# Second layer: dispatch and projections in one stage, the dispatch cut into pieces between the half chunks

## The chip, the cores and the metric

The kernel runs on one core of one Trainium2 chip. The metric is the device time of one execution in microseconds, the median of three runs. Five engines have queues of their own and meet only at semaphores: PE (TensorE, matmuls), DVE (VectorE), ACT (ScalarE), POOL (GpSimd) and SP (SyncE, which issues most DMAs). "SPq" and "PEq" in the rows are the queues of the engines, in which issues and waits stand.

## What is computed

A block of four layers over 4 batches of 1024 tokens with 128 features; each layer is x + s * g, s an attention-like part and g an activated feed-forward part, both of the normalized x. The change lies in the second layer (L1), in what comes first there: the projections of the attention, and the router of the feed-forward part with 8 experts, of which each token takes two.

```python
qkv = x @ W_qkv + b_qkv                       # attention, 16 heads of 8
q, k, v = jnp.split(qkv, 3, axis=2)
...
logits = xf @ Wg + bg                         # feed-forward, xf = x as 4096 rows
w = jax.nn.softmax(logits, axis=-1)
top_w, top_idx = jax.lax.top_k(w, K)          # K = 2 of 8
top_w = top_w / (top_w.sum(axis=-1, keepdims=True) + EPS_GATE)
```

## The kernel before

The kernel is a row of stages. Each (`Stage`) has its own buffers and semaphores and ends with a barrier of all engines, so that nothing of the next begins before the last DMA of the stage has landed. x is held as 32 tiles of 128 tokens, its normalized form turned as `xnT` (128 features by 4096 tokens).

**dispatch1** (`dispatch_stage`, L1789) reads `xnT` and writes three maps to memory: where each row goes (`send`), its weight (`pick_weight`) and the expert of each block of 128 rows (`owner`). SP loads the router's weights, then stores 4.7 MB of zeros over `sorted_x`, from a tile that DVE clears and into which GpSimd writes row numbers. PE makes 32 tiles of logits, each with 128 columns of `xnT` as weights and only 8 moving columns. DVE does all else in one chain (`link`: each instruction waits for the one before): softmax with ACT's Exp, comparison of every pair of experts (five instructions over 2048 elements, L1900 to L1905), a mask, then a wait for two matmuls of PE that count the mask, then running sums over the tiles, slots, weights and owners. SP stores the maps:

```python
            sp.wait_ge(zeroed, NZ * DMA)
            for n, (dst, src) in enumerate(((send_d, send_i), (weight_d, wsel), (expert_d, owner_i))):
                sp.wait_ge(maps_ready, n + 1)
                sp.dma_start(dst[:], src[:]).then_inc(stored, DMA)
...
            for t in range(NT):
                last = mm(lg[:, t, :], xnT[:, t * P:(t + 1) * P], wr[:], start=True, stop=True)
            last.then_inc(logits, 1)
            pe.wait_ge(mask_ready, 1)
```

**proj1** (`project_l1`, L2160) makes q, k and v. A chunk is 512 tokens; PE makes three fills for each, q, k and v (24 in all), into a ring of four PSUM slots. q and k are stored as three bf16 parts whose sum is the float value. Per half chunk m (q or k of a chunk, 16 in all): ACT writes the first part (`first_part`), DVE the remainder (`remainder`, L2247), ACT the second part of it (`second_part`), DVE the third (`third_part`, L2254). v only gets its bias on DVE (`values`, L2258). PE may fill a slot again when ACT and DVE have read it. SP stores q, k and v for each batch of two chunks, ten DMAs a batch. The next stage, attn1, starts with loads of q and k.

Of the kernel before, what the change touches and what calls it, by code (L numbers as in the profile page):

```python
# [7 lines left out]
I32 = mybir.dt.int32  # L8
# [5 lines left out]
P = 128  # L14
D = 128
# [885 lines left out]
def broadcast_rows(vec, n=P):  # L901

    return vec.partition_broadcast(n)
# [1256 lines left out]
def project_l1(nc, xnT, w_qkv, b_qkv, q_d, k_d, v_d):  # L2160
# [4 lines left out]
    SLOTS = 4  # L2165
    with Stage(nc, "proj1") as st:
        w, b_col, bv_b = st.sb("w", [P, 3 * D]), st.sb("b_col", [P, 2]), st.sb("bv_b", [P, D])
# [4 lines left out]
        consts, made, high, rested, middle, low, v_ready, stored = (  # L2172
            st.sem(n) for n in ("consts", "made", "high", "rested", "middle", "low", "v_ready", "stored"))
        block = st.block()

        @block.sync
        def _(sp):
            sp.dma_start(w[:], w_qkv).then_inc(consts, DMA)
# [16 lines left out]
            sp.wait_ge(stored, DMA * n)  # L2195

        @block.tensor
        def _(pe):
            pe.wait_ge(consts, 4 * DMA)
            for n in range(N):  # L2200
# [8 lines left out]
                if j < 2:  # L2209
                    last = nc.tensor.matmul(ps[:, n % SLOTS, :], w[:, j * D:(j + 1) * D], xnT[:, c * CH:(c + 1) * CH],  # L2210
                                            start=True, stop=True)
                else:
                    for t in range(TPC):
                        last = nc.tensor.matmul(ps[:, n % SLOTS, t * P:(t + 1) * P], xnT[:, (c * TPC + t) * P:(c * TPC + t + 1) * P],
                                                w[:, 2 * D:3 * D], start=True, stop=True)
                last.then_inc(made, 1)

        @block.scalar
        def _(act):
            def first_part(m):  # L2220
                c, j = divmod(m, 2)
                act.wait_ge(made, 3 * c + j + 1)
# [10 lines left out]
            for m in range(2 * NCH):  # L2233
                if m + 1 < 2 * NCH:
                    first_part(m + 1)
                second_part(m)

        @block.vector
        def _(dve):
            V = nc.vector  # L2240

# [14 lines left out]
            def values(c):  # L2256
                dve.wait_ge(made, 3 * c + 3)
# [3 lines left out]
            dve.wait_ge(consts, 4 * DMA)  # L2261
            remainder(0)
            for m in range(2 * NCH):
# [4 lines left out]
                third_part(m)  # L2268

# [756 lines left out]
def recurrent_block_kernel(nc, a, out):  # L3026
# [15 lines left out]
    with ExitStack() as ctx:  # L3042
# [33 lines left out]
        dispatch(1, "top2", BLOCKS, "Wg bg")  # L3076
        project_l1(nc, xnT, a["L1_attn_W_qkv"], a["L1_attn_b_qkv"], q1, k1, v1)
# [41 lines left out]
```

## Time and profile before

| | us |
|---|---|
| median of three runs | 3577.64 (3575.88 to 3577.95) |
| profiled execution, time | 3574.13 |
| its span | 3572.4 |
| dispatch1, SP's first issue to that of proj1 | 1859.69 to 1911.32 |
| proj1, to SP's first issue of attn1 | 1911.32 to 1959.42 |

Times in the rows are microseconds from the start of the span. PE is busy for 80% of the span, DVE for 66%, ACT for 52%, GpSimd for 42%. In a row of the timeline, the brackets say how long the engine had stood idle before the row and what it had waited for; "x8" is a number of instructions, merged into one row. A float32 matmul stands twice in the trace.

### The profile page before, as it was taken

Reading aid. Unit: us, or ns where it says so; the run is one execution under the profiler, and the core shown is the slowest. Engines: PE = TensorE matmul, PEld = TensorE weight load, DVE = VectorE, ACT = ScalarE, POOL = GpSimd, SP = SyncE. Lnnn points to the kernel's source line nnn. Section 1 sums busy time; section 2 is a strip of 40 time slices with the busy share of each in tenths; the row PEclk is TensorE's granted clock in tenths of the full one; section 3 lists DMA queues with packets and bytes.
Section 4 is the critical chain, followed back from the end, with each engine's and each line's share of the span. In section 5 each row is a group of like instructions: output and inputs, shape, how many; then the busy total and the mean of one; then the engine's idle time right before and its main releaser. Section 6 shows DMA issues by size and latency. Waiting matters only on the chain. (4 is left out here: it accounts for less than half of the span.)

```text
span 3572.4 us, 66799 instructions
## 1 busy us (share of the span) xinstructions
PE 2857.9 (80%) x21131; PEld 1282.4 (36%) x21132; DVE 2354.1 (66%) x3384; ACT 1843.7 (52%) x2985; POOL 1515.6 (42%) x1109
## 2 busy tenths in 40 slices
PE   3999999999999978599943799999969820384993
PEld 1333333333333328333331122222246520252771
DVE  5666666666666637788866999999823358134663
ACT  2555555555555540344462599999934350144431
POOL 0989989999998980100000010110126604560000
PEclk9999999999999988799966799999989955696995
DMA  2011111111111115200013222222121123113002
GB/s 83 30 45 42 54 41 46 54 41 46 49 46 46 40 45 202 85 1 0 0 55 103 42 58 50 53 53 54 46 83 46 36 79 115 40 40 87 10 12 64
DMA packets 265381, 189.65 MB, mean 53 GB/s; under 512 B 149056, under 2 KB 210872, under 8 KB 264322
## 3 DMA queue, kind: packets, MB, share of 16 engines
q1 hardware_dynamic: 257154, 174.25, 17.2%
q0 software_dynamic: 8128, 14.18, 1.2%
q8 instruction: 50, 0.82, 0.1%
q14 instruction: 49, 0.40, 0.0%
HBM read 105.28 MB, written 67.62 MB: 48 GB/s over the span
## 5 line engine op out<-in xcount | busy, mean ns | idle before, releaser
L331 POOL TENSOR_TENSOR attn_esum<-attn_esum,attn_prob 128x1024 f32<-128x1024 f32 x384 | 904.0, 2354 | 31.1 <-ACT attn_prob L482 7.4
L553 DVE TENSOR_REDUCE attn_half_max<-attn_peek 128x2 f32<-128x1024 f32 x512 | 627.4, 1225 | 399.1 <-PE attn_peek L382 395.3
L482 ACT ACTIVATE attn_prob<-attn_score 128x1024 f32<-128x1024 f32 x512 | 512.4, 1021 | 247.8 <-PE attn_score L365 247.8
L848 ACT ACTIVATE attn_prob<-attn_score 128x512 f32<-128x512 f32 x1024 | 556.3, 596 | 72.1 <-PE attn_score L798 58.0
L865 DVE TENSOR_REDUCE attn_half_max<-attn_peek 128x2 f32<-128x1024 f32 x512 | 583.6, 1217 | 10.8 <-PE attn_peek L784 10.7
L412 PE MATMUL attn_acc<-attn_prob,attn_v 128*64 128x512 f32 x2048 | 487.9, 597 | 0.1
L814 PE MATMUL attn_acc<-attn_prob,attn_v 128*32 128x256 f32 x4096 | 327.8, 392 | 12.0 <-ACT attn_out L840 10.5
L1779 POOL DMA_INDIRECT sorted_x<-attn_sent_rows,attn_send x64 | 62.6, 978 | 555.0 <-PE attn_score L798 520.3
L784 PE MATMUL attn_peek<-attn_ke,attn_qe 48*128 48x512 bf16 x1024 | 202.8, 393 | 47.0 <-DMA attn_ke<-k 32.3
L382 PE MATMUL attn_peek<-attn_hi 64*128 64x512 f16 x1024 | 200.2, 388 | 34.2 <-DVE attn_half_max L553 34.2
L798 PE MATMUL attn_score<-attn_qe,attn_ke 49*128 49x512 bf16 x1024 | 200.6, 389 | 7.7 <-ACT attn_prob L848 5.8
L2134 DVE TENSOR_TENSOR experts_pre<-experts_up,experts_b 128x512 f32<-128x512 f32 x112 | 77.5, 692 | 193.8 <-PE experts_up L2064 193.8
L331 POOL TENSOR_TENSOR attn_esum<-attn_prob 128x1024 f32<-128x1024 f32 x64 | 151.1, 2361 | 126.7 <-ACT attn_prob L482 126.7
L412 PEld LDWEIGHTS attn_acc<-attn_prob,attn_v 128*64 128x64 f32 x2048 | 130.8, 137 | 201.0 <-issue 156.4
L1583 PE MATMUL experts_up<-experts_x,experts_up_w 128*128 (+1 forms) x816 | 198.3, 379 | 1.5 <-DVE experts_down_w L1672 1.5
L367 PE MATMUL attn_score<-attn_hi 64*128 64x512 f16 x1024 | 195.1, 378 | 0.0
L367 PE MATMUL attn_score<-attn_lo,attn_hi 64*128 64x512 f16 x1024 | 195.1, 378 | 0.0
L367 PE MATMUL attn_score<-attn_hi,attn_lo 64*128 64x512 f16 x1024 | 194.9, 377 | 0.0
L365 PE MATMUL attn_score<-attn_shift,attn_sel 64*128 64x512 bf16 x1024 | 194.8, 377 | 0.0
L1845 POOL MEMSET dispatch_before<- 128x64 f32 x2 | 0.3, 151 | 457.9 <-POOLq L41 457.9
L1649 ACT ACTIVATE experts_a<-experts_up 128x512 f32<-128x512 f32 x136 | 81.2, 597 | 157.0 <-PE experts_up L1583 154.0
L2034 POOL DMA_INDIRECT picked<-experts_y,experts_result x112 | 115.7, 1033 | 88.0 <-POOL experts_y L2031 85.3
(451 smaller groups left out, 4539.0 us busy)
## 6 DMA issues: line engine op xcount, KB each, us to landing
attn_xb<-attn_x_all SPq DMA_DIRECT2D x66, 256.0 KB, 2.5
attn_invB<-inv SPq DMA_DIRECT2D x64, 256.0 KB, 3.9
o<-attn_out SPq DMA_DIRECT2D x32, 512.0 KB, 2.7
out_o<-o SPq DMA_DIRECT2D x8, 2048.0 KB
mix_f<-picked SPq DMA_DIRECT2D x16, 512.0 KB, 7.2
experts_x<-sorted_x SPq DMA_DIRECT2D x112, 65.0 KB
attn_qe<-q SPq DMA_DIRECT2D x192, 32.0 KB
attn_ke<-k SPq DMA_DIRECT2D x192, 32.0 KB
```

The source lines that it names most:

```text
L331: nc.gpsimd.tensor_tensor(own, before, prob[:, u % NPROB, :, :], ALU.add).then_inc(added, 1)
L367: last = mm(score[:, u % 2, h, :], ks[r, slot, WHICH["k"], keys], qs[r, slot, WHICH["q"], queries], start=(n == 0), stop=False)
L382: last = mm(peek[:, h, :], hi[r, slot, WHICH["q"], t * P:(t + 1) * P], hi[r, slot, WHICH["k"], half * CH:(half + 1) * CH], start=True, sto ...
L412: last = mm(acc[rows_of(h), :], v[:, slot, t, rows_of(h)], prob[:, u % NPROB, h, :], start=(t == 0), stop=(t == KT - 1))
L482: nc.scalar.activation(prob[:, u % NPROB, :, :], score[:, u % 2, :, :], ACT.Exp).then_inc(exped, 1)
L553: V.tensor_reduce(half_max[:, half, :, t], peek[:], AX.X, ALU.max, negate=True).then_inc(maxed, 1)
L784: last = mm(peek[:, m % NPEEK, n, :], qe[r, slot, pair, t * P:(t + 1) * P], ke[r, slot, pair, half * CH:(half + 1) * CH], start=True, stop ...
L798: last = mm(score[:, (PAIR * k + n) % RING, :], ke[r, slot, pair, t * P:(t + 1) * P], qe[r, slot, pair, c * CH:(c + 1) * CH], start=True, ...
L814: last = mm(acc[h * COL:(h + 1) * COL, cols], v[:, slot, t, h, :], prob[:, (HG * s + h) % NPROB, cols], start=(t == 0 and p == 0), stop=(t ...
L848: nc.scalar.activation(prob[:, n % NPROB, :], score[:, n % RING, :], ACT.Exp).then_inc(exped, 1)
L865: V.tensor_reduce(half_max[:, half, PAIR * pair:PAIR * (pair + 1), t], peek[:, m % NPEEK, :, :], AX.X, ALU.max, negate=True).then_inc(maxe ...
L1583: ins = nc.tensor.matmul(out, ws[pw][:, cols], xs[px][own], start=start and n == 0, stop=stop and n == 2)
```

## The change

`dispatch1` and `proj1` become one stage, `dispatch_and_project_stage`; the second dispatch of the kernel (third layer) stays as it was. SP loads both sets of weights, the projection's first, stores the zeros, then q, k and v as before. GpSimd clears the tile of zeros and, from its own queue, stores the three maps. On PE the logit tiles stand in four pieces of eight, each followed by a fill, and the two counting matmuls in front of fill 12. ACT's Exp follows the second part of half chunk 2. DVE's work of the dispatch is cut into eight pieces, which are the old instructions in nearly the old order (the weights come before the running sums, the slots after them); between them stand one or two steps of the projection.

```diff
 
-def project_l1(nc, xnT, w_qkv, b_qkv, q_d, k_d, v_d):
+def dispatch_and_project_stage(nc, xnT, w, bias, blocks, xs_d, send_d, weight_d, expert_d, w_qkv, b_qkv, q_d, k_d, v_d):
...
         @block.sync
+            sp.dma_start(wq[:], w_qkv).then_inc(consts, DMA)
             for j in range(2):
                 sp.dma_start(b_col[:, j:j + 1], column(b_qkv[j * D:(j + 1) * D])).then_inc(consts, DMA)
             sp.dma_start(bv_b[:], broadcast_rows(b_qkv[2 * D:3 * D])).then_inc(consts, DMA)
+            sp.dma_start(wr[:], w).then_inc(router_in, DMA)
+            sp.dma_start(bias_b[:], broadcast_rows(bias)).then_inc(router_in, DMA)
+            sp.wait_ge(zero_made, 2)
+            for n in range(NZ):
+                sp.dma_start(xs_d.rearrange("(n p r) d -> n p (r d)", n=NZ, p=P)[n], zero[:].rearrange("p r d -> p (r d)")).then_inc(zeroed, DMA)
...
+            sp.wait_ge(zeroed, NZ * DMA)
             sp.wait_ge(stored, DMA * n)
+
+        @block.gpsimd
+        def _(pool):
+            nc.gpsimd.memset(zero[:], 0.0).then_inc(zero_made, 1)
+            pool.wait_ge(zero_made, 1)
+            nc.gpsimd.iota(zero[:, :, D:D + 1].bitcast(I32), [[0, blocks // NZ], [0, 1]], base=NOWHERE, channel_multiplier=0
+                           ).then_inc(zero_made, 1)
...
+            pool.wait_ge(built, 4)
...
+            for n, (dst, src) in enumerate(((send_d, send_i), (weight_d, wsel), (expert_d, owner_i))):
+                pool.wait_ge(maps_ready, n + 1)
+                pool.dma_start(dst[:], src[:]).then_inc(maps_stored, DMA)
+            pool.wait_ge(maps_stored, 3 * DMA)
 
...
+            def fill(n):
...
+            def score_tiles(h):
+                for t in range(h * NT // 4, (h + 1) * NT // 4):
+                    last = mm(lg[:, t, :], xnT[:, t * P:(t + 1) * P], wr[:], start=True, stop=True)
+                if h == 3:
+                    last.then_inc(logits, 1)
+
+            def count():
+                pe.wait_ge(built, 6)
+                pe.wait_ge(mask_ready, 1)
+                flat = mask[:].rearrange("p t e -> p (t e)")
+                mm(ranked[:, 0, :, :].rearrange("p t e -> p (t e)"), earlier[:], flat, start=True, stop=True)
+                mm(tallied[:, 0, :, :].rearrange("p t e -> p (t e)"), ones[:], flat, start=True, stop=True).then_inc(counted, 1)
+
+            pe.wait_ge(consts, 4 * DMA)
+            for n in range(3):
+                fill(n)
+            pe.wait_ge(router_in, 2 * DMA)
+            for h in range(4):
+                score_tiles(h)
+                fill(3 + h)
+            for n in range(7, N):
+                if n == 12:
+                    count()
+                fill(n)
 
         @block.scalar
         def _(act):
             def first_part(m):
                 c, j = divmod(m, 2)
-                act.wait_ge(made, 3 * c + j + 1)
+                act.wait_ge(filled, 3 * c + j + 1)
                 nc.scalar.activation(part[0][:, j, c * CH:(c + 1) * CH], ps[:, (3 * c + j) % SLOTS, :], ACT.Identity, bias=b_col[:, j:j + 1]
                                      ).then_inc(high, 1)
 
@@ -2234,10 +2311,19 @@
                 if m + 1 < 2 * NCH:
                     first_part(m + 1)
                 second_part(m)
+                if m == 2:
+                    act.wait_ge(shifted_ready, 1)
+                    nc.scalar.activation(score[:], shifted[:], ACT.Exp).then_inc(exped, 1)
...
+            def scores():
+
+                dve.wait_ge(router_in, 2 * DMA)
+                dve.wait_ge(logits, 1)
+                link(V.tensor_tensor(score[:], lg[:], per_expert(bias_b), ALU.add))
+                link(V.reduce_max(red[:], score[:], AX.X))
+                V.tensor_tensor(shifted[:], score[:], per_tok(red), ALU.subtract).then_inc(shifted_ready, 1)
...
+            def softmax():
+                dve.wait_ge(built, 6)
+                dve.wait_ge(exped, 1)
+                link(V.reduce_sum(red[:], score[:], AX.X))
...
+            def equals():
+                link(V.tensor_tensor(pair2[:], sj, si, ALU.is_equal))
...
+            def larger():
+                link(V.tensor_tensor(pair[:], sj, si, ALU.is_gt))
...
+            def ranks():
+                link(V.reduce_sum(rank[:], pair[:], AX.X))
+                V.tensor_scalar(mask[:], rank[:], 2.0, None, ALU.is_lt).then_inc(mask_ready, 1)
+                dve.wait_ge(mask_ready, 1)
+
+            def weights():
+                link(V.tensor_tensor(weight[:], mask[:], score[:], ALU.mult))
...
+                for j in range(2):
...
+            def places():
+
+                dve.wait_ge(counted, 1)
...
+            def slots(a):
...
+                V.tensor_copy(send_i[:], slot[:]).then_inc(maps_ready, 2)
+
+            def owners():
...
+                V.tensor_copy(owner_i[:], owner[:]).then_inc(maps_ready, 1)
+
+            def step(m):
                 if m % 2 == 1:
                     values(m // 2)
                 if m + 1 < 2 * NCH:
                     remainder(m + 1)
                 third_part(m)
+
+            dve.wait_ge(consts, 4 * DMA)
+            remainder(0)
+            for m in range(2):
+                step(m)
+            scores()
+            for m in range(2, 4):
+                step(m)
+            softmax()
+            step(4)
+            equals()
+            step(5)
+            larger()
+            step(6)
+            ranks()
+            for m in range(7, 9):
+                step(m)
+            weights()
+            for m in range(9, 11):
+                step(m)
+            a = places()
+            for m in range(11, 13):
+                step(m)
+            slots(a)
+            step(13)
+            owners()
+            for m in range(14, 16):
+                step(m)
...
-        dispatch(1, "top2", BLOCKS, "Wg bg")
-        project_l1(nc, xnT, a["L1_attn_W_qkv"], a["L1_attn_b_qkv"], q1, k1, v1)
+        dispatch_and_project_stage(nc, xnT, *inputs("L1_ffn_", "Wg bg"), BLOCKS, sorted_x, send, pick_weight, owner,
+                                   a["L1_attn_W_qkv"], a["L1_attn_b_qkv"], q1, k1, v1)
```

PE, start of the stages: the logits (`lg`), the counts (`ranked`, `tallied`) and fills (`ps`) in the kernel before.

```order
L1865 MATMUL dispatch_lg<-dispatch_wr,xnT 128x8 x32
L1869 MATMUL dispatch_ranked<-dispatch_mask,dispatch_earlier 128x256
L1870 MATMUL dispatch_tallied<-dispatch_mask,dispatch_ones 128x256
L39 UNCONDITIONAL_BRANCH
L2197 UNCONDITIONAL_BRANCH
L2210 MATMUL proj_ps<-xnT,proj_w 128x512 x2
L2214 MATMUL proj_ps<-proj_w,xnT 128x128 x4
```

The same place now, to the fills behind the last logit tiles:

```order
L2263 MATMUL proj_ps<-xnT,proj_wq 128x512 x2
L2266 MATMUL proj_ps<-proj_wq,xnT 128x128 x4
L2272 MATMUL proj_lg<-proj_wr,xnT 128x8 x8
L2263 MATMUL proj_ps<-xnT,proj_wq 128x512
L2272 MATMUL proj_lg<-proj_wr,xnT 128x8 x8
L2263 MATMUL proj_ps<-xnT,proj_wq 128x512
L2272 MATMUL proj_lg<-proj_wr,xnT 128x8 x8
L2266 MATMUL proj_ps<-proj_wq,xnT 128x128 x4
L2272 MATMUL proj_lg<-proj_wr,xnT 128x8 x8
L2263 MATMUL proj_ps<-xnT,proj_wq 128x512 x2
```

Three fills stand before the first logit tiles, three more between the pieces; the barrier is gone.

DVE around the mask, before: the last comparison result, the mask, then the running sums that read the counts.

```order
L1905 TENSOR_REDUCE dispatch_rank<-dispatch_pair 128x256
L1906 TENSOR_SCALAR dispatch_mask<-dispatch_rank 128x256
L1911 MEMSET dispatch_place 128x8
L1912 COPY dispatch_place<-dispatch_tallied 128x248
L1915 COPY dispatch_place<-dispatch_place 128x8
```

DVE around the mask now, to the first instruction of the weights:

```order
L2372 TENSOR_REDUCE proj_rank<-proj_pair 128x256
L2373 TENSOR_SCALAR proj_mask<-proj_rank 128x256
L2344 TENSOR_TENSOR proj_v<-proj_ps,proj_bv_b 128x512
L2333 SCALAR_TENSOR_TENSOR proj_rest<-proj_ps,proj_b_col,proj_part 128x512
L2340 TENSOR_TENSOR proj_part<-proj_rest,proj_part 128x512
L2333 SCALAR_TENSOR_TENSOR proj_rest<-proj_ps,proj_b_col,proj_part 128x512
L2340 TENSOR_TENSOR proj_part<-proj_rest,proj_part 128x512
L2377 TENSOR_TENSOR proj_weight<-proj_mask,proj_score 128x256
```

Steps 7 and 8 of the projection stand behind the mask, and their first remainder (half chunk 8) reads fill 12, which stands behind the counts on PE.

## Rows read from the trace of the kernel before

**Rows 1.** Windows: stretch, us; PE, PEld, DVE, ACT, POOL busy (instructions); clock, DMA share, GB/s

```profile
1859.69:1959.42 99.73, 42.02 (x164) 29.72 (x164) 56.34 (x97) 21.02 (x34) 1.32 (x7) 0.62 0.44 136
1863.96:1876.50 12.54, 12.54 (x59) 12.46 (x59) 0.00 (x0) 0.00 (x0) 0.00 (x0) 0.50 0.88 359
...
1925.60:1958.70 33.10, 16.11 (x67) 8.79 (x66) 20.42 (x32) 14.19 (x24) 0.00 (x0) 0.79 0.94 254
```

**Rows 2.** Windows of 1 us, columns as above; the clock's mean of 0.5 and 1.0

```profile
1921.00:1922.00 1.00, 1.00 (x4) 0.52 (x3) 1.00 (x2) 0.00 (x0) 0.00 (x0) 0.94 0.00 0
...
1945.00:1946.00 1.00, 0.00 (x0) 0.00 (x0) 1.00 (x3) 0.51 (x1) 0.00 (x0) 0.50 1.00 338
...
3467.00:3468.00 1.00, 0.90 (x5) 0.90 (x6) 0.04 (x1) 0.35 (x1) 0.00 (x0) 0.67 0.00 0
```

**Rows 3.** Timeline: start us, us, engine, line, operation; PE's last matmuls before both falls

```profile
1941.68 1.13 PE L2214 MATMUL proj_ps<-proj_w,xnT 128*128 128x128 f32 x8 [0.22 <-DVE proj_rest L2247]
...
3462.38 0.60 PE L2576 MATMUL linattn_late<-identity,linattn_z 128*64 128x128 f32 x4
```

**Rows 4.** Timeline of the dispatch stage

```profile
1859.69 0.33 SPq L1832 DMA_DIRECT2D dispatch_wr<-in_L_ffn_Wg  x1
...
1862.69 13.82 PE L1865 MATMUL dispatch_lg<-dispatch_wr,xnT 128*128 128x8 f32 x64 [4.86 <-DMA dispatch_bias_b<-in_L_ffn_bg]
...
1876.63 0.42 DVE L1890 TENSOR_TENSOR dispatch_score<-dispatch_lg,dispatch_bias_b 128x256 f32<-128x256 f32 x1 [13.19 <-PE dispatch_lg L1865]
...
1891.72 1.22 PE L1869 MATMUL dispatch_ranked<-dispatch_mask,dispatch_earlier 128*128 128x256 f32 x2 [15.21 <-DVE dispatch_mask L1906]
...
1893.94 0.07 DVE L1911 MEMSET dispatch_place<- 128x8 f32 x1 [2.27 <-PE dispatch_tallied L1870]

```

**Rows 5.** Timeline of the projection stage, its start and full-clock fills

```profile
1915.59 3.78 PE L2210 MATMUL proj_ps<-xnT,proj_w 128*128 128x512 f32 x4 [21.79 <-DMA proj_bv_b<-in_L_attn_b_qkv]
...
1918.57 0.75 DVE L2247 SCALAR_TENSOR_TENSOR proj_rest<-proj_ps,proj_b_col,proj_part 128x512 f32<-128x512 f32 x1 [9.22 <-ACT proj_part L2223]
1919.16 1.92 PE L2214 MATMUL proj_ps<-proj_w,xnT 128*128 128x128 f32 x8
...
1925.32 1.05 PE L2214 MATMUL proj_ps<-proj_w,xnT 128*128 128x128 f32 x8
...
1929.54 1.98 PE L2210 MATMUL proj_ps<-xnT,proj_w 128*128 128x512 f32 x4
```

**Rows 6.** Timeline, DVE: the same remainder one chunk apart, and values

```profile
1932.12 0.68 DVE L2258 TENSOR_TENSOR proj_v<-proj_ps,proj_bv_b 128x512 f32<-128x512 f32 x1
...
1932.72 0.74 DVE L2247 SCALAR_TENSOR_TENSOR proj_rest<-proj_ps,proj_b_col,proj_part 128x512 f32<-128x512 f32 x1
...
1936.03 0.74 DVE L2247 SCALAR_TENSOR_TENSOR proj_rest<-proj_ps,proj_b_col,proj_part 128x512 f32<-128x512 f32 x1
```

**Rows 7.** Timeline: SP's issues of the first and last batch, DVE's last, the next stage

```profile
1925.60 1.31 SPq L2188 DMA_DIRECT2D q<-proj_part  x3
...
1927.46 1.32 SPq L2188 DMA_DIRECT2D k<-proj_part  x3
...
1928.83 3.93 SPq L2192 DMA_DIRECT2D v<-proj_v  x4
...
1945.97 0.68 DVE L2254 TENSOR_TENSOR proj_part<-proj_rest,proj_part 128x512 bf16<-128x512 f32 x1
1948.74 1.58 SPq L2188 DMA_DIRECT2D q<-proj_part  x3
...
1952.33 4.20 SPq L2192 DMA_DIRECT2D v<-proj_v  x4
1959.42 4.09 SPq L696 DMA_DIRECT2D attn_qe<-q  x12
```

**Rows 8.** Lines of GpSimd: busy us, mean ns; a memset and plain DMAs of other stages

```profile
L759 POOL MEMSET attn_v<- 128x2048 f32 x1 | 1.8, 1804 | 96.3 <-POOLq L41 96.3
...
L2531 POOL DMA_DIRECT2D linattn_raw<-in_L_ffn_sw x3 | 1.7, 596 | 54.5 <-POOLq L41 54.5
```

More of the change, by code:

```diff
@@ L2165, in project_l1 @@
     SLOTS = 4
+    E = 8
+    NZ = 4
     with Stage(nc, "proj1") as st:
[L2167 removed]
+        wq, b_col, bv_b = st.sb("wq", [P, 3 * D]), st.sb("b_col", [P, 2]), st.sb("bv_b", [P, D])
         rest = st.sb("rest", [P, 2, CH])
@@ L2170, in project_l1 @@
         v = st.sb("v", [P, NT, D])
-        ps = st.ps("ps", [P, SLOTS, CH])
-        consts, made, high, rested, middle, low, v_ready, stored = (
-            st.sem(n) for n in ("consts", "made", "high", "rested", "middle", "low", "v_ready", "stored"))
+        zero = st.sb("zero", [P, blocks // NZ, ROW])
+        wr, bias_b = st.sb("wr", [P, E]), st.sb("bias_b", [P, E])
+        full = [P, NT, E]
+        four = [P, NT, E, E]
+        score, shifted, mask, hot, weight, rank, place, place2 = (
+            st.sb(n, full) for n in ("score", "shifted", "mask", "hot", "weight", "rank", "place", "place2"))
+        pair, pair2 = st.sb("pair", four), st.sb("pair2", four)
+        before = st.sb("before", [P, E, E])
+        earlier, ones = st.sb("earlier", [P, P]), st.sb("ones", [P, P])
+        red = st.sb("red", [P, NT])
+        count, room, start, end = (st.sb(n, [P, E]) for n in ("count", "room", "start", "end"))
+        begun = st.sb("begun", [P, E, NT])
+        spread = st.sb("spread", [P, E, E])
+        slot, wsel = st.sb("slot", [P, 2, NT]), st.sb("wsel", [P, 2, NT])
+        send_i = st.sb("send_i", [P, 2, NT], I32)
+        first_i, first = st.sb("first_i", [P, blocks], I32), st.sb("first", [P, blocks])
+        past, owner, owner_i = st.sb("past", [1, blocks, E]), st.sb("owner", [1, blocks]), st.sb("owner_i", [1, blocks], I32)
+        ps = st.ps("ps", [P, SLOTS, CH])
+        lg = st.ps("lg", [P, NT, E])
+        ranked, tallied = st.ps("ranked", [P, 2, NT, E]), st.ps("tallied", [P, 2, NT, E])
+        names = ("consts", "made", "high", "rested", "middle", "low", "v_ready", "stored")
+        consts, filled, high, rested, middle, low, v_ready, stored = (st.sem(n) for n in names)
+        names = ("router_in", "built", "zero_made", "zeroed", "logits", "shifted_ready", "exped", "route_step", "mask_ready", "counted",
+                 "maps_ready", "maps_stored")
+        (router_in, built, zero_made, zeroed, logits, shifted_ready, exped, route_step, mask_ready, counted, maps_ready, maps_stored) = (
+            st.sem(n) for n in names)
         block = st.block()
@@ new lines, in slots @@
+            def slots(a):
+                for j in range(2):
+                    link(V.tensor_scalar(hot[:], rank[:], float(j), None, ALU.is_equal))
+                    link(V.tensor_tensor(shifted[:], hot[:], a[:], ALU.mult))
+                    link(V.reduce_sum(slot[:, j, :], shifted[:], AX.X))
+                V.tensor_copy(send_i[:], slot[:]).then_inc(maps_ready, 2)
+            def owners():
+                link(V.tensor_tensor(past[:], over(first[0:1, :].unsqueeze(2), [1, blocks, E]),
+                                     end[0:1, :].unsqueeze(1).to_broadcast([1, blocks, E]), ALU.is_ge))
+                link(V.reduce_sum(owner[:], past[:], AX.X))
+                link(V.tensor_scalar(owner[:], owner[:], E - 1.0, None, ALU.min))
+                V.tensor_copy(owner_i[:], owner[:]).then_inc(maps_ready, 1)
```

65 lines of the change are left out of this document (53 added, 12 removed).

## Prediction

> **What bounds the kernel now.** The whole kernel is a chain of stages with a barrier behind each, so I read the window table first, for the two stages that are merged. From SP's first issue of the dispatch stage (1859.69) to SP's first issue of the attention stage (1959.42) are 99.7 us, in which DVE is busy for 56.3 and PE for 42.0 [rows 1]. No engine is full: the reader is to see a path that changes hands. The timeline gives it. In the dispatch stage PE turns out the 32 tiles of logits for 13.8 us while DVE stands still; then DVE works alone from 1876.63 to 1909.34 (its idle 9.22 us end at 1918.57), 32.7 us, with 2.3 us in it for the hand-over to PE and back [rows 4, 5]. Between that and DVE's first instruction of the projections at 1918.57 lie 9.2 us: the landing of the map, a barrier, the loads of the projection weights, the first matmul [rows 4, 5]. The projections run at DVE's pace, 3.31 us for a chunk of 512 tokens [rows 6]. DVE ends at 1946.65, but the stage lasts until 1959.42: SP is still issuing stores, and the DMA engines, 94% busy from the first store on, are behind [rows 1, 7]. By these rows the stages cost 16.9 (to the logits) + 32.7 + 9.2 + 28.1 + 12.8 = 99.7 us.
>
> **Part 1: start, up to the logits.** In the new stage the loads of the projection come first. In the old projection stage PE started 4.3 us after SP's first issue, and I take the same. Three fills follow: 5.5 us (1915.59 to 1921.08) [rows 5]. Then come four pieces of eight logit tiles, 13.8 us together as in the dispatch stage, with three fills between them: two of q/k at 1.8 (3.57 us for two) and one of v at 1.9, all at half clock, 5.5 us. Logits: 4.3 + 5.5 + 13.8 + 5.5 = 29.1 us behind the start, against 16.9 before. GpSimd now clears the 2340 columns of zero (1.80 us for 2048 [rows 8], so 2.1 against DVE's 2.0), under SP's six loads; nothing on the path. The zero stores may delay the bias load by some tenths.
>
> The clock decides here. The logit tiles alone kept PE busy without a gap and its clock stayed at 0.50, which is 1.2 GHz; the dense matmuls of the projections brought 1.00 (2.4 GHz) 5.5 us after their start [rows 1, 2, 5]. So I expect 1.00 about when the three fills are over. It outlives dense work: by 2.2 us behind the last matmul of the projections (1942.81 to 1945.0), by 4.3 us behind 3462.98 [rows 2, 3]. I take 3.4 us, between the two; each microsecond at full clock does the work of two at half clock, so the logits come at 29.1 - 3.4 = **25.7 us**. The later fills are too thin between the logit tiles to raise it again, as I read it. The ends: never at full clock before the logits, 29.1; always, 20.4 (4.3 + 5.5 + 64 tile passes at 0.12 = 7.7, where a pass of v with its load takes 1.05/8 = 0.13 [rows 5], + two fills at 1.98/2 + one at 1.05, 2.9 together).
>
> **Part 2: DVE from the logits to its end.** The first two half chunks (and one remainder more) are done while PE makes logits: this is the overlap that the change buys. What remains is serial on DVE. The dispatch pieces: 32.7 - 2.3 = 30.4 us [rows 4]; the clearing is GpSimd's now. Steps 2 to 15 of the projection: seven chunks at 3.31, less the remainder of step 2, 0.75: 22.4 us [rows 6]. The small cast and the hand-over to ACT's Exp (below 0.5) stay in the sum; the step behind scores hides the latter.
>
> **Part 3: the wait that is added.** The two counting matmuls stand in front of fill 12, and wait for the mask; remainder 8 on DVE needs fill 12. When the mask is ready, DVE has only values(3) to do. PE then counts (2.2 us from mask to result), fills and hands on through ACT (2.98 us from the first matmul of a stage to the first remainder), less the 0.68 of values(3): **4.5 us** of stall, at half clock, since PE will have had nothing to do for some 10 us [rows 4, 5, 6]. At full clock it would be about half, 2.3. Behind the waiting count stand all fills from 12 on, and ACT behind them. That is more than the 2.3 us of waiting that the old stage had at the count. For the other steps PE is up to four fills ahead and refills its slots while DVE does a piece, so I cost them at nothing; without that cover each would cost up to 2.98.
>
> **Part 4: the tail.** Before, SP was 2.1 us behind with q of the last batch (1948.74 against 1946.65 for the last DVE write) and took 7.8 us for q, k and v. Now DVE needs some 16 us for a batch of four steps (57.3 us for 14 steps, parts 2 and 3), and the stores of the batch before are long out. q of the last batch may go when step 14 is done, 1.2 us before DVE ends; issues cost 1.31 + 1.32 + 3.93 = 6.6 as in the first batch, then 2.9 us pass to the next stage's first issue [rows 7]. From DVE's end: 0.1 + 6.6 + 2.9 - 1.2 = **8.4 us** (12.8 before). The DMA engines' own work, 0.94 x 33.1 / 4 = 7.8 us a batch [rows 1], gives 8.2, so neither end is far; with the old 7.8 us of issues it would be 9.6. The three maps go to GpSimd's queue, where a plain DMA costs 0.58 us of issue [rows 8], and the last of them is ready some 3 us before DVE ends: nothing on the path. Here a rule of the Trainium skill speaks against the change (SBUF — State Buffer, SBUF: two separate sides): DMAs issued by GpSimd need a port for their descriptors that some DVE instructions hold. No row of the kernel before shows such DMAs beside such DVE work; if the rule bit, the sum would grow by what the last rival gives.
>
> **Sum.** 25.7 + 30.4 + 22.4 + 4.5 + 8.4 = 91.4 us against 99.7: **8.3 us less**. The profiled execution has a span of 3572.4 and a time of 3574.13, the median of the runs is 3577.64; against the profiled one that is 3565.8, against the median **3569.3**. The rest of the kernel is unchanged, and the attention stage begins with the same idle PE as before.
>
> **Rivals.**
> *A, the clock doesn't rise before the logits, or falls at once.* For it: the thin logit tiles left it at 0.50 for 13.8 us, and the two clock rows are single cases. Against it: the same three fills in the same order did bring it up. 94.8 us, 4.9 less: 3572.7, within the bound.
> *B, the clock stays up through the logits* (and perhaps for the count). For it: fills stand between the tiles now, and 4.3 us were outlived once. Against it: the tiles take most of the time. 86.1 us, 13.6 less: 3564.0, and 3561.8 with the count at full clock.
> *C, every half chunk pays the hand-over (slower).* PE may refill a slot only when DVE has made the remainder from it; if the pieces hold the remainders back so far that PE and ACT stand idle and DVE then waits for both, each of the 14 steps pays up to 2.98 us less DVE's own work beside it. From 0.6 us a step the gain is gone, from 1.1 us it is slower by over 7.2 us; at 1.5 us, 21 us more than forecast, 3590. Against it: four slots hold two and a half half chunks with their values, and a piece is 2 to 7 us long, time for one to four fills even at half clock.
> *D, the maps end the stage.* If GpSimd can only write them when DVE is quiet, three issues of 0.6 and one landing follow DVE's end. That the landing is longer than the 2.9 us behind SP's last store is what it needs; with 10 us it ends at 11.8 instead of 8.4, 3.4 us more: 3572.7. The rule of the page named above would work this way.
>
> **How the numbers follow.** Forecast 0.44, A 0.26, B 0.21, C 0.05, D 0.04. A measurement of this kernel tells about 0.2%, 7.2 us, from no change, and the forecast's 8.3 lies just beyond. The terms of the forecast move by about 1.5 us (clock after the fills, pace of the steps with less waiting, tail 8.2 to 9.6), so I give a quarter of it to "same". Faster: 0.33 + 0.21 + some of A = 0.60; same 0.11 + most of A and D, 0.34; slower 0.06 with what I have not seen. The range, 3562 to 3574, reaches from B with the fast count to just past A and D; C is left out, with a little at either end.
>
> **What would show it.** In the changed kernel's rows: first fill 4.3 us behind SP's first issue; the last logit tile at 25 to 26 us, with a stretch at 1.00 in the middle; the eight-tile pieces at 3.4 us in half clock and near 2 in full; DVE's add of the logit bias right behind; a wait of DVE of about 4 us before the remainder behind the mask, and none over 0.5 us elsewhere; DVE's end near 83 us, the next stage's first issue near 91. Rival A shows logits at 29, B at 20 to 22, C waits of DVE <- ACT before many remainders, D a GpSimd store that lands last. The prediction is wrong in its mechanism if DVE has long waits after the logits other than the one at the count, or if the end is not set by SP's stores.

## Result, and the profile after

The changed kernel took 3565.49 us (median of 6 runs, 3560.68 to 3570.26), the kernel before 3575.98 us (6 runs, 3572.85 to 3577.95). The ratio is 0.9971 with a 95% interval of 0.9961 to 0.9981: faster by 10.5 us or 0.29%, more than the 0.2% that can be told from no change; the interval's upper edge, 0.19% faster, lies at that bound. Forecast were 3569.3 us and a range of 3562 to 3574. The profiled execution took 3567.24 us (span 3565.2, clock 0.902), against 3574.13 before.

The windows of the merged stage in the changed kernel (columns as in [rows 1]), then single microseconds at the rise and fall of the clock:

```profile
1859.41:1950.25 90.84, 48.20 (x164) 33.59 (x164) 54.19 (x96) 21.22 (x34) 5.24 (x11) 0.63 0.49 149
...
1869.00:1870.00 1.00, 1.00 (x8) 1.00 (x6) 1.00 (x3) 0.00 (x0) 0.00 (x0) 0.55 1.03 431
1870.00:1871.00 1.00, 1.00 (x11) 1.00 (x10) 0.25 (x1) 0.00 (x0) 0.00 (x0) 1.00 0.91 384
...
1873.00:1874.00 1.00, 1.00 (x8) 1.00 (x8) 0.98 (x2) 0.51 (x1) 0.00 (x0) 0.65 1.03 431
1874.00:1875.00 1.00, 1.00 (x3) 0.74 (x4) 0.37 (x1) 0.00 (x0) 0.00 (x0) 0.50 0.59 234
```

The stage lasts 90.84 us where [rows 1] had 99.73 for the two. PE is busier than before (48.2 against 42.0 us) though it does the same matmuls: more of them fall in half clock. The clock goes to 1.00 (2.4 GHz) at about 1869.9, 6.1 us behind PE's start, and is back at 0.50 (1.2 GHz) at about 1873.3, after 3.4 us, while PE is busy without a pause.

The timeline of the changed kernel, in three parts: to the logits, around the count, and the end. It answers to [rows 4, 5, 7].

```profile
1859.41 0.33 SPq L2204 DMA_DIRECT2D proj_wq<-in_L_attn_W_qkv  x1
...
1863.77 3.78 PE L2263 MATMUL proj_ps<-xnT,proj_wq 128*128 128x512 f32 x4 [6.21 <-DMA proj_bv_b<-in_L_attn_b_qkv]
...
1869.04 2.26 PE L2272 MATMUL proj_lg<-proj_wr,xnT 128*128 128x8 f32 x16
...
1872.10 2.31 PE L2272 MATMUL proj_lg<-proj_wr,xnT 128*128 128x8 f32 x16
...
1876.11 3.42 PE L2272 MATMUL proj_lg<-proj_wr,xnT 128*128 128x8 f32 x16
...
1881.23 3.42 PE L2272 MATMUL proj_lg<-proj_wr,xnT 128*128 128x8 f32 x16
1884.76 0.42 DVE L2351 TENSOR_TENSOR proj_score<-proj_lg,proj_bias_b 128x256 f32<-128x256 f32 x1 [10.39 <-PE proj_lg L2272]
...
1906.43 0.29 DVE L2373 TENSOR_SCALAR proj_mask<-proj_rank 128x256 f32<-128x256 f32 x1
...
1906.87 1.19 PE L2280 MATMUL proj_ranked<-proj_mask,proj_earlier 128*128 128x256 f32 x2 [14.02 <-DVE proj_mask L2373]
...
1908.70 2.95 PE L2263 MATMUL proj_ps<-xnT,proj_wq 128*128 128x512 f32 x4
...
1910.65 0.69 ACT L2300 ACTIVATE proj_part<-proj_ps,proj_b_col 128x512 bf16<-128x512 f32 x1 [12.30 <-PE proj_ps L2263]
...
1911.38 0.75 DVE L2333 SCALAR_TENSOR_TENSOR proj_rest<-proj_ps,proj_b_col,proj_part 128x512 f32<-128x512 f32 x1 [3.93 <-ACT proj_part L2300]
...
1939.87 1.31 SPq L2219 DMA_DIRECT2D q<-proj_part  x3
...
1940.37 0.67 DVE L2340 TENSOR_TENSOR proj_part<-proj_rest,proj_part 128x512 bf16<-128x512 f32 x1
1941.23 1.74 SPq L2219 DMA_DIRECT2D k<-proj_part  x3
...
1943.01 4.12 SPq L2223 DMA_DIRECT2D v<-proj_v  x4
1950.25 4.08 SPq L696 DMA_DIRECT2D attn_qe<-q  x12
```

The reader is to see three stretches. From SP's first issue to DVE's first use of the logits are 25.35 us. From there to DVE's end at 1941.04 are 56.28, with one wait of 3.93 in them. From there to the next stage's first issue are 9.21. Of the kernel before the same three are 16.94, 70.02 and 12.77 [rows 4, 7]. The change thus costs 8.4 us in the first, and takes 13.7 from the second and 3.6 from the third: 8.9 together. What lies outside the stage took 3474.4 us before and 3476.4 here.

This table holds the three stretches of all profiled executions that are told of below, so that each edit can be read where it acts. "Outside" is the time of the execution less the stage; nothing is changed there, and it alone goes from 3472.3 to 3479.8.

| kernel | to logits | to DVE's end | tail | stage | outside | median, ratio to before with interval |
|---|---|---|---|---|---|---|
| before | 16.94 | 70.02 | 12.77 | 99.73 | 3474.4 | 3575.98 |
| changed | 25.35 | 56.28 | 9.21 | 90.84 | 3476.4 | 3565.49, 0.9971 (0.9961 to 0.9981) |
| changed, a0_after | 19.01 | 56.29 | 9.21 | 84.51 | 3474.4 | 3565.60, 0.9972 (0.9963 to 0.9982) |
| changed, a1_after | 25.32 | 56.27 | 9.27 | 90.86 | 3479.8 | 3565.43, 0.9968 (0.9955 to 0.9982) |
| e1_count15 | 25.32 | 52.27 | 9.24 | 86.83 | 3478.7 | 3560.98, 0.9962 (0.9953 to 0.9972) |
| e2_maps_sp | 25.31 | 56.29 | 9.22 | 90.82 | 3479.0 | 3565.88, 0.9975 (0.9964 to 0.9985) |
| e3_serial | 18.97 | 58.32 | 12.79 | 90.08 | 3473.6 | 3565.22, 0.9974 (0.9963 to 0.9986) |
| e4_together | 20.28 | 60.36 | 9.24 | 89.88 | 3477.1 | 3564.92, 0.9969 (0.9959 to 0.9980) |
| e5_v_first | 25.33 | 56.36 | 6.36 | 88.05 | 3477.5 | 3561.61, 0.9963 (0.9950 to 0.9976) |
| e6_all_three | 20.28 | 56.41 | 6.34 | 83.03 | 3476.6 | 3558.88, 0.9952 (0.9939 to 0.9966) |
| e7_before_pool_maps | 16.94 | 71.09 | 12.75 | 100.78 | 3475.4 | 3574.22, 0.9999 (0.9989 to 1.0008) |
| e8_warm | 21.29 | 56.27 | 9.21 | 86.77 | 3477.0 | 3559.74, 0.9959 (0.9945 to 0.9972) |
| e9_all_and_warm | 19.44 | 56.41 | 6.36 | 82.21 | 3473.7 | 3556.08, 0.9950 (0.9937 to 0.9964) |
| e10_split_warm | 22.83 | 52.45 | 6.74 | 82.02 | 3472.3 | 3555.43, 0.9943 (0.9930 to 0.9957) |

### The profile page after: what moved, and what is told of

It reads as the page before. It is cut to its first block and busy times, and to the rows that moved or that the text cites. A ratio compares the mean times of both kernels' runs of the same rounds, so it can differ in the third digit from the quotient of the medians.

```text
span 3565.2 us, 66780 instructions
## 1 busy us (share of the span) xinstructions
PE 2867.8 (80%) x21131; PEld 1286.5 (36%) x21132; DVE 2351.7 (66%) x3383; ACT 1844.4 (52%) x2985; POOL 1521.0 (43%) x1113
## 5 line engine op out<-in xcount | busy, mean ns | idle before, releaser
L865 DVE TENSOR_REDUCE attn_half_max<-attn_peek 128x2 f32<-128x1024 f32 x512 | 583.7, 1215 | 11.7 <-PE attn_peek L784 11.7
L814 PE MATMUL attn_acc<-attn_prob,attn_v 128*32 128x256 f32 x4096 | 328.3, 392 | 12.0 <-ACT attn_out L840 10.5
L1649 ACT ACTIVATE experts_a<-experts_up 128x512 f32<-128x512 f32 x136 | 81.3, 598 | 157.2 <-PE experts_up L1583 154.2
```

The source lines that it names most:

```text
L814: last = mm(acc[h * COL:(h + 1) * COL, cols], v[:, slot, t, h, :], prob[:, (HG * s + h) % NPROB, cols], start=(t == 0 and p == 0), stop=(t ...
L865: V.tensor_reduce(half_max[:, half, PAIR * pair:PAIR * (pair + 1), t], peek[:, m % NPEEK, :, :], AX.X, ALU.max, negate=True).then_inc(maxe ...
```

## Experiments

The theory under test: the time is the sum of start to logits, DVE's serial work with one wait, and a tail of SP's stores; the clock shortens the first. The rivals: the gain comes from the interleaving and not from the merging; the maps on GpSimd's queue matter; the tail is the DMA engines'.

### The changed kernel again: the clock goes two ways

> The changed kernel, unchanged, as the measure for the runs beside it. Expected: the merged stage (SP's first issue to that of the attention stage) 90.8 us again, within 1 us, and DVE's wait before the remainder behind the mask 3.9 us. If the length came from the chance of when the clock rises, it would differ by 2 to 5 us.

> The changed kernel once more, for the clock: in one profile of it the full clock began 6.1 us behind TensorE's first matmul of the stage and lasted 3.4 us (logits after 25.4 us), in the other 3.1 us behind and lasted 10.6 us (logits after 19.0 us). If the first is the rule, as in four of five kernels so far, logits after 25 to 26 us and a stage of 90.8; if chance decides evenly, either.

The first of them had a stage of 84.51 us, not 90.8. Its clock and its logits:

```profile
1864.00:1865.00 1.00, 1.00 (x2) 0.45 (x2) 0.11 (x1) 0.69 (x1) 0.00 (x0) 0.54 1.06 440
1865.00:1866.00 1.00, 1.00 (x9) 0.79 (x8) 0.64 (x1) 0.59 (x2) 0.00 (x0) 1.00 1.04 440
1874.00:1875.00 1.00, 1.00 (x13) 1.00 (x11) 0.00 (x0) 0.10 (x1) 0.00 (x0) 1.00 0.02 9
1875.00:1876.00 1.00, 1.00 (x8) 1.00 (x7) 0.00 (x0) 0.00 (x0) 0.00 (x0) 0.58 0.00 0
```
```profile
1857.59 0.33 SPq L2204 DMA_DIRECT2D proj_wq<-in_L_attn_W_qkv  x1
...
1876.60 0.43 DVE L2351 TENSOR_TENSOR proj_score<-proj_lg,proj_bias_b 128x256 f32<-128x256 f32 x1 [5.58 <-PE proj_lg L2272]
...
1942.10 4.08 SPq L696 DMA_DIRECT2D attn_qe<-q  x12
```

A mean of 0.54 or 0.58 in a microsecond puts the change inside it: full clock from 1864.92, 3.0 us behind PE's start at 1861.90, to 1875.16, so 10.2 us (the 10.6 in the expectations that name it was read too long), nearly to the last logit tile. The logits came after 19.01 us, 6.3 earlier; the other two stretches are the same to 0.1 us. a1_after repeated the first profile: rise 5.8 us behind PE's start, 3.4 us at full clock by a row of 0.94, two of 1.00 and one of 0.77, stage 90.86. So the same program meets either case; what decides between them isn't known. The 6.3 us are half of the 12 over which the runs of this kernel spread (3558 to 3571).

### e3_serial: merging without interleaving

```diff
             pe.wait_ge(consts, 4 * DMA)
-            for n in range(3):
-                fill(n)
             pe.wait_ge(router_in, 2 * DMA)
             for h in range(4):
                 score_tiles(h)
-                fill(3 + h)
-            for n in range(7, N):
-                if n == 12:
+            for n in range(N):
+                if n == 4:
                     count()
                 fill(n)
```
DVE then runs all pieces of the dispatch first, and all 16 half chunks after them; ACT's Exp stands first on ACT.

> One stage as in the changed kernel, with GpSimd's part, but nothing of the two overlaps on DVE: first the whole dispatch, then the projections; PE makes all logit tiles first and the counts before fill 4. Theory 1 (what the merging saves is mostly the end of one stage and the start of the next): logits at 18.7, dispatch 30.4 and 2.3 for the count, projections 27 to 28, tail 12.8 as before: 91.2 to 92.3 us, only 0.4 to 1.5 more than the changed kernel. Theory 2 (the overlap is what brings the gain): at least 96 us.

```profile
1864.46 13.79 PE L2272 MATMUL proj_lg<-proj_wr,xnT 128*128 128x8 f32 x64 [6.88 <-DMA proj_bias_b<-in_L_ffn_bg]
...
1878.40 0.42 DVE L2347 TENSOR_TENSOR proj_score<-proj_lg,proj_bias_b 128x256 f32<-128x256 f32 x1 [26.93 <-PE proj_lg L2272]
...
1894.65 1.06 PE L2281 MATMUL proj_tallied<-proj_mask,proj_ones 128*128 128x256 f32 x2
...
1898.04 0.07 DVE L2387 MEMSET proj_place<- 128x8 f32 x1
...
1936.04 0.68 DVE L2336 TENSOR_TENSOR proj_part<-proj_rest,proj_part 128x512 bf16<-128x512 f32 x1
...
1942.22 4.22 SPq L2223 DMA_DIRECT2D v<-proj_v  x4
1949.51 4.08 SPq L696 DMA_DIRECT2D attn_qe<-q  x12
```

The stage is 90.08 us and the median 3565.22: the same as the changed kernel in its profile with the late clock and in the median, within 1 us. Beside a0_after's 84.51 it is 5.6 longer: e3_serial's clock stood at 0.50 through all its logit tiles (13.79 us), and it has only one profile. The rival (96 or more) is out. Beside the kernel before, the middle is 11.7 us shorter and the rest 2.0 longer. The middle lost the 9.2 us between the dispatch and the first remainder of [rows 5], since four fills stand ready when the dispatch is over, and the 2.3 us at the count, since DVE now makes the weights between the mask and the first use of the counts: they were ready at 1895.71, DVE came for them at 1898.04. Beside the changed kernel with the late clock, interleaving costs 6.4 us until the logits and gives 2.0 in the middle and 3.6 in the tail: nothing in the sum. It gives something in the tail because with the half chunks packed at the end the stores of earlier batches are still going out when DVE ends, as in [rows 7]: 12.79 us.

### e1_count15: the wait at the count

```diff
-                if n == 12:
+                if n == 15:
                     count()
```

> The changed kernel with the two counting matmuls in front of fill 15 instead of fill 12. Theory (the added wait is only the order on PE): fills 12 to 14 need nothing from behind the mask, so DVE finds its remainder ready, the wait of 3.9 us goes, and the stage lasts 86.9 us. Rival (PE at half clock has just been idle, and DVE would wait for a fill anyway): a wait of 2 us or more stays, the stage lasts over 88.5 us.

The wait of 3.93 us is gone, and the middle is 4.0 us shorter (52.27), the other stretches unchanged. Fills 12 to 14 are made before the mask is there, so DVE finds its input; the result of the count is wanted only later. The median is 4.6 us below a0_after's. The timeline of e1_count15:

```profile
1906.47 1.19 PE L2280 MATMUL proj_ranked<-proj_mask,proj_earlier 128*128 128x256 f32 x2 [1.24 <-DVE proj_mask L2373]
...
1935.96 0.67 DVE L2340 TENSOR_TENSOR proj_part<-proj_rest,proj_part 128x512 bf16<-128x512 f32 x1
```

PE, idle for 14.02 us before the count in the changed kernel, is idle for 1.24 here: it has worked ahead. DVE ends 77.6 us behind the stage's start instead of 81.6.

### e4_together: logit tiles in one run

```diff
             for h in range(4):
                 score_tiles(h)
-                fill(3 + h)
-            for n in range(7, N):
+            for n in range(3, 7):
+                fill(n)
+            for n in range(7, N):
...
-            for m in range(2):
-                step(m)
+            step(0)
             scores()
+            step(1)
```

> All 32 logit tiles stand directly behind the first three fills on TensorE, instead of a fill behind each eight; VectorE takes the dispatch's first piece after one half chunk instead of two. Theory 1 (the merged stage's time is start to logits, then VectorE's serial work, then the stores of the last batch): the logits come three fills of half clock earlier less what the clock gives, so logits 20 to 22 us behind the stage's start instead of 25.4, the stretch from the logits to VectorE's end 58 us (one step more behind them, 1.6), tail 9.2: stage 88.4 us in an execution whose clock behaves as in the profiled one of the changed kernel, 2.4 less. Theory 2 (interleaved fills are free cover): no change, 90.8. In executions in which the clock stays up through the logits, the gain is halved.

```profile
1872.12 10.56 PE L2272 MATMUL proj_lg<-proj_wr,xnT 128*128 128x8 f32 x64
...
1885.34 0.75 DVE L2334 SCALAR_TENSOR_TENSOR proj_rest<-proj_ps,proj_b_col,proj_part 128x512 f32<-128x512 f32 x1 [0.61 <-ACT proj_part L2301]
...
1887.05 0.75 DVE L2334 SCALAR_TENSOR_TENSOR proj_rest<-proj_ps,proj_b_col,proj_part 128x512 f32<-128x512 f32 x1 [0.36 <-ACT proj_part L2301]
...
1889.87 0.75 DVE L2334 SCALAR_TENSOR_TENSOR proj_rest<-proj_ps,proj_b_col,proj_part 128x512 f32<-128x512 f32 x1 [0.87 <-ACT proj_part L2301]
```

The logits come after 20.28 us as expected, 5.1 earlier. But the middle grows by 4.1 (expected 1.7). The step that now stands behind the logits (values, a remainder and a third part) is 2.0 of it, and the other 2.05 are new waits of 0.61, 0.36, 0.87 and 0.21 us, since PE has made no fill ahead. The stage gains 1.0 of the 2.4 us. The median doesn't tell the two apart (3564.92 and 3565.60).

### e5_v_first: what the tail is

```diff
+                if b == BATCH - 1:
+                    store_v()
                 for j, dst in enumerate((q_d, k_d)):
...
             step(13)
+            values(7)
             owners()
```
store_v holds SP's four stores of v; step 15 no longer makes the last values.

> In the last batch the values are made before the owners' map and SP stores v first, then q and k. Theory 1 (SP's own issues, 1.3 + 1.7 + 4.1 us behind VectorE's end, set the tail of 9.2 us): v's issues go beside VectorE's last pieces and the tail is 3.1 (k's issue and landing) + 3 = about 6.0: stage 87.6 us, 3.2 less. Theory 2 (the tail is the DMA engines' work, about 7.8 us a batch): the tail stays above 8, the stage at 90 or more.

```profile
1930.58 8.06 SPq L2219 DMA_DIRECT2D v<-proj_v  x8
...
1938.22 1.46 DVE L2345 TENSOR_TENSOR proj_part<-proj_rest,proj_part 128x512 bf16<-128x512 f32 x2
...
1938.92 1.61 SPq L2227 DMA_DIRECT2D q<-proj_part  x3
1940.57 2.11 SPq L2227 DMA_DIRECT2D k<-proj_part  x3
1946.04 4.07 SPq L696 DMA_DIRECT2D attn_qe<-q  x12
```

The tail falls from 9.21 to 6.36. The issues of v (8.06 us for two batches' eight) now lie beside DVE's work; behind DVE's end at 1939.68 stand only the end of q's issue, that of k, and 3.4 us of landing and hand-over.

This shows that v's stores behind DVE's end made 2.8 us of the tail, but not that SP's issues set it rather than the DMA engines. Moving v takes its bytes out of the tail as well as its issues, so the DMA engines' theory too would have it shorter, and the bound of 8 us in the expectation didn't allow for that. The windows speak for neither alone: the DMA engines (the share in front of the last number) were busy for 0.93 of the time from 1941 to 1949 in the changed kernel and throughout from 1940 to 1944.5 in e5_v_first, each time until 1.3 to 1.5 us before the next stage began.

The changed kernel, then e5_v_first:

```profile
1941.00:1949.00 8.00, 0.00 (x0) 0.00 (x0) 0.04 (x1) 0.00 (x0) 0.00 (x0) 0.50 0.93 249
1949.00:1950.25 1.25, 0.00 (x0) 0.00 (x0) 0.00 (x0) 0.00 (x0) 0.00 (x0) 0.50 0.00 0
```
```profile
1940.00:1944.50 4.50, 0.00 (x0) 0.00 (x0) 0.00 (x0) 0.00 (x0) 0.00 (x0) 0.50 1.07 369
1944.50:1946.04 1.54, 0.00 (x0) 0.00 (x0) 0.00 (x0) 0.00 (x0) 0.00 (x0) 0.50 0.03 8
```

Which of the two sets the tail stays open; a run that thins out the issues and leaves the bytes would tell.

### e2_maps_sp and e7_before_pool_maps: the queue that writes the maps

In e2_maps_sp the three stores of maps stand on SP's queue ahead of the last batch instead of on GpSimd's. In e7_before_pool_maps the kernel before is changed in this alone, the other way:

```diff
+            if not capacity:
+                for n, (dst, src) in enumerate(((send_d, send_i), (weight_d, wsel), (expert_d, owner_i))):
+                    pool.wait_ge(maps_ready, n + 1)
+                    pool.dma_start(dst[:], src[:]).then_inc(stored, DMA)
```

> The changed kernel with the three maps stored by SP, in front of the stores of the last batch, instead of by GpSimd. Theory (the queue of the maps is worth nothing, since SP waits there anyway: the last map is ready some 1.5 us before q of the last batch): the stage lasts 90.8 us, within 0.5. Rival (GpSimd's queue is part of the gain): at least 0.9 us longer, three more issues of 0.3 on SP's path.

> The kernel before, with only the three maps of the first dispatch moved from SP's queue to GpSimd's. Theory (the queue that writes the maps is worth nothing by itself; the gain is the merging): the two stages together 99.7 to 100.3 us, median within 1 us of the kernel before. Rival (GpSimd's DMAs collide with VectorE's work): the landing of the maps is later by 1 us or more, the stages 101 or more.

```profile
1910.44 0.19 DVE L1972 CAST dispatch_owner_i<-dispatch_owner 1x72 int32<-1x72 f32 x1
1910.92 0.56 POOL L1863 DMA_DIRECT2D owner<-dispatch_owner_i  x1 [1.27 <-DVE dispatch_owner_i L1972]
1913.70 0.34 SPq L2184 DMA_DIRECT2D proj_w<-in_L_attn_W_qkv  x1
```

The kernel before at the same place:

```profile
1909.16 0.18 DVE L1966 CAST dispatch_owner_i<-dispatch_owner 1x72 int32<-1x72 f32 x1
1909.38 0.24 SPq L1840 DMA_DIRECT2D owner<-dispatch_owner_i  x1
1911.32 0.36 SPq L2178 DMA_DIRECT2D proj_w<-in_L_attn_W_qkv  x1
```

In the merged stage the queue makes no difference: 90.82 against 90.84 us. Where the last map ends a stage, as in the kernel before, GpSimd's queue costs: from the end of the cast (1910.63) to the next stage's first issue are 3.07 us, against 1.98 with SP's (1909.34 to 1911.32). The stretch grew by 1.1 us, and the 100.78 us of both stages lie between the expected 100.3 and the rival's 101. The landing was later by the 1 us that the rival asked for, but not by a collision: DVE stood idle from the cast on. The median doesn't show it (ratio 0.9999, 0.9989 to 1.0008).

### e6_all_three: do the savings add?

Count in front of fill 15, tiles together, v first.

> Count in front of fill 15, logit tiles together, v of the last batch first. If the three savings lie in different parts of the stage, they add: 90.8 - 3.9 - 2.4 - 3.2 = 81.3 us of stage, and a median of about 3556 (3565.6 - 9.5). If the stage has a floor (VectorE's serial work 53 us, start and end of 30), one of them is partly lost: 83 to 85 us, 3558 to 3560.

83.03 us, 7.8 less than the changed kernel; alone the three gave 4.0, 1.0 and 2.8, which is 7.8 too. They add; the expected 81.3 was too low by what e4_together and e5_v_first fell short of their own. The stage and the median, 3558.88, are those that the expectation gave to the rival (83 to 85, 3558 to 3560), but not for its reason: no saving is partly lost here, each saving is that of the single edit to 0.1 us.

### e8_warm, e9_all_and_warm, e10_split_warm: dense work ahead of the stage's own

```diff
+            for n in range(4):
+                mm(ps[:, 0, :], xnT[:, 0:P], xnT[:, 0:CH], start=True, stop=True)
             pe.wait_ge(consts, 4 * DMA)
```
These matmuls stand where PE waits for the weights; the first fill overwrites what they leave. e10_split_warm has three of them, with count 15 and v first, and the tiles left between fills.

> The changed kernel with four dense matmuls of 128x512 more in front of TensorE's first wait, while it stands idle for the weights; what they write is overwritten by the first fill. Theory 1 (the full clock comes a fixed 6 us of dense work behind the start): it comes some 4 us earlier, about when the first fill is made, and the logits come earlier: by 2 us if it lasts 3.4 us again, by 5 to 6 if it lasts through the tiles as in the profile with the early rise; stage 85 to 89 instead of 90.8. Theory 2 (the thin logit tiles decide, not when the dense work began): the stretch of full clock only moves forward, logits at 25 us, stage within 1 us of 90.8.

```profile
1859.44 5.37 PE L2284 MATMUL proj_ps<-xnT 128*128 128x512 f32 x8 [1.91 <-PEq L41]
1864.65 1.88 PE L2263 MATMUL proj_ps<-xnT,proj_wq 128*128 128x512 f32 x4
...
1872.55 2.90 PE L2272 MATMUL proj_lg<-proj_wr,xnT 128*128 128x8 f32 x16
```

The fills ahead of the tiles ran at full clock (1.88 us for the first two against 3.78), the logits came after 21.29 us instead of 25.35, and nothing else moved: stage 86.77, median 5.7 us below a1_after's. The clock had risen 3.4 us behind the first of the four and lasted 10.2 us. Theory 1 holds in direction, though not with its 6 us. One profile couldn't show it, since a0_after had an early rise without these matmuls; but all three kernels with them had one, 3.4, 4.2 and 3.5 us behind their first matmul, and of the eight profiles without them whose fills stand first only a0_after did. The four matmuls were too long by 0.9 us (the first fill began 5.27 us behind SP's first issue, not 4.36).

> The same four matmuls in the kernel with the count in front of fill 15, the logit tiles together and v first. Theory 1: logits at 16 to 18.5 us instead of 20.3, stage 79 to 81 instead of 83.0, median 1.5 to 4 us below 3558.9. Theory 2: no change, 83 us.

82.21 us against 83.03: 0.8 of the 2 to 4 expected. The full clock lasted 6.8 us and fell 2.8 us into the unbroken run of tiles, which took 11.09 us here and 10.55 in e6_all_three. So the early matmuls moved the full clock forward to where fewer tiles were behind it; theory 2 is nearer for this order.

> Three edits that paid so far, with the logit tiles left between fills as in the changed kernel: count in front of fill 15, v of the last batch first, and three dense matmuls (instead of four) in front of TensorE's first wait. Theory (dense fills between the tiles keep the full clock that the early matmuls brought, and the savings lie in different parts): logits 20.4 us behind the stage's start, 52.4 from there to VectorE's end, tail 6.4: stage 79.2 us, against 82.2 with all tiles together and four matmuls; median about 3554. Rival (with a pause between the early matmuls and the first fill, or with less dense work, the clock falls again after 3.4 us): logits at 23 to 25, stage 82 to 84, median 3557 to 3559.

82.02 us, 2.8 above the theory's 79.2 and at the lower end of the rival's 82 to 84: the clock rose after 3.5 us and lasted 6.8, not the rival's 3.4, so the logits came after 22.83. The middle was as expected (52.45) and the tail 0.3 longer (6.74). The median is 3555.43, ratio 0.9943 (0.9930 to 0.9957): the fastest version tried, some 10 us below the changed kernel, though not told apart from e9_all_and_warm and e6_all_three by the intervals.

## Why the prediction was right, point by point

**What bounds.** Right: the stage is start, DVE's work and tail in turn, as the three stretches show: e8_warm moved only the first, e1_count15 only the second, e5_v_first only the third.

**Part 1, to the logits: 25.7 forecast, 25.35 measured.** Each piece came as read from the rows: PE's start 4.36 us behind SP's first issue (4.3), the three fills 5.27 (5.5), the clock's rise 0.9 us behind their end, 3.4 us at full clock (3.4). That the last value fits is luck: it was taken between two single cases, 2.2 and 4.3, without a reason for it. It was met in the profiles of the changed kernel twice of three times; the third is rival B. GpSimd's clearing and the zero stores held up nothing.

**Part 2 and 3: 57.3 forecast, 56.28 measured.** The wait was 3.93 us (4.5), and it is the only one above 0.1 us behind the logits. Both pieces of it were a little shorter than their rows: fill 12 began 1.98 us behind the end of the mask (2.2 was to the result of the counts, which a fill doesn't need), and the remainder came 2.68 us behind the fill's start (2.98). The clock had no part in it, being at half until fill 12 was made (the row of 2.95 us holds fills 12 and 13). DVE's work itself was 52.35 (52.8).

**Part 4: 8.4 forecast, 9.21 measured.** The term was undersized. The order was right, q going 1.17 us ahead of DVE's end. But I took the issue costs from the first batch: k took 1.74 us and v 4.12, where [rows 7] had 1.32 and 3.93, and 3.1 us passed behind the last issue instead of 2.9. In these rows an issue behind other stores in flight costs more, and the last batch's would have told so. The other sum for the tail, by the DMA engines' work, gave 8.2 and was short as well; which of the two sets the tail is open, as e5_v_first says.

**Sum.** 91.4 forecast, 90.84 measured for the stage, 8.3 and 8.9 us less. The median fell by 10.5. Of the 1.6 us between, executions with the early clock, 6.3 us shorter each, are a likely part; since the share of such executions wasn't counted and the rest of the kernel varies by 7.5 us, this is argued, not shown.

**Where the reason was wrong.** I wrote that the overlap of the first half chunks with the logits is what the change buys. e3_serial says no: without any of it the stage is 0.8 us shorter than in the profiled execution of the changed kernel, and the medians are the same. The overlap takes 4.05 us of DVE's work (two steps and a remainder, by [rows 6]) ahead of the logits and delays the logits by 6.4. What pays without interleaving is the landing, the barrier, the loads and the first matmul that lie between the two stages before, 9.2 us, and the weights' new place, 2.3, less 2.0 for the later logits. In the changed kernel interleaving costs 6.4 us before the logits and gives back 2.0 and 3.6. It is not worthless in itself: its middle holds the wait at the count, 3.9 us, and with that gone e1_count15 has 86.83 us, 3.3 less than e3_serial, though its clock rose late (medians 3560.98 and 3565.22). The sum held because it priced both sides from rows.

**The rivals.** A (94.8 us) was not seen; all profiles of the changed kernel had a full clock before the logits. B (logits at 20 to 22, stage 86.1) happened in one of three, at 19.01 and 84.51, lower than priced since the first three fills too ran faster (the later three add to 3.0 us by [rows 5], not 2.9). C: no wait but the one at the count, so four slots are enough while a piece lies between. D: the maps' queue changed nothing in the merged stage: GpSimd issued the last of them at 1938.87, 2.2 us before DVE's end, with DVE busy throughout, in 0.56 us, as in [rows 8]. The rule of the Trainium skill behind it (SBUF — State Buffer, SBUF: two separate sides) holds such DMAs back beside some DVE instructions only. The trace shows no hold, but whether the instructions beside these three issues are of that kind no run here shows, so it doesn't speak against the rule.

## What to carry to other kernels

Price a merge of two stages by the hand-over that goes (here 9.2 us of landing, barrier, loads and first matmul), and price interleaving on its own: work that is put ahead of a long-awaited result delays it by its length on the engine that makes the result (6.4 us here, for 4.05 us of DVE's work). A wait for a result stands best as late in an in-order queue as its consumer allows: moving one line by three fills gave 4.0 us. In a tail of stores, store first what is ready first: 2.8 us here, whether it was the issues or the bytes.

## What the runs showed of the hardware

- The same program met two clock histories in one stage: full clock from 3.0 us behind PE's first matmul for 10.2 us, or from 5.8 to 6.1 us for 3.4 us. That is 6.3 us of 90.
- Full clock outlives dense work by different spans under thin tiles: it fell 2.8 us into an unbroken run of tiles of 128x8 (e9_all_and_warm), and lasted 10.2 us in all where a fill stood between every eight (e8_warm, a0_after), but 3.4 us (a1_after) and 6.8 us (e10_split_warm) with the same order in other profiles. What sets the span was not found. At full clock eight tiles took 1.85 us, at half clock 3.42.
- DMA engines were busy for 0.97 of the 11.35 us from DVE's end to 1958.0 in the kernel before, and for 0.93 of 1941 to 1949 in the changed one.
- Issues on SP grow when others are in flight: three stores of k cost 1.30 to 1.34 us in the first batches, 1.74 behind q in the last, 2.11 right behind eight stores of v.
- A plain DMA on GpSimd's queue cost 0.56 to 0.79 us to issue and, at the end of a stage, 1.1 us more than on SP's until the next stage began.
